# All weighted tiles of a deformable convolution summed on VectorE, partly out of PSUM, before TensorE folds them

## The reference, cut to what matters

```python
x = x + _L0_conv_ref(_gn(x), ...)   # Winograd convolution with weights of 6x6 frequencies
x = x + _L1_conv_ref(_gn(x), ...)   # offsets by a 3x3 convolution, then a deformable 3x3 convolution
x = x + _L2_conv_ref(_gn(x), ...)   # four convolutions with binary weights, activations of 8 bits
x = x + _L3_conv_ref(_gn(x), ...)   # 3x3 convolution + edge convolution, channel attention
```

```python
def qhtanh(x):
    return jnp.clip(ste_round(jnp.clip(x, -10.0, 10.0) / HT_SCALE), -127.0, 127.0) * HT_SCALE
out01 = qhtanh(out01) + qhtanh(identity0)
x_b1l0 = qhtanh(out01) + qhtanh(op1)
```

```python
diff_v = xp[:, :, :-2, :] - xp[:, :, 2:, :]
edge_out = jnp.einsum('oc,bchw->bohw', W_edge, jnp.abs(diff_v))
```

## Time and profile before

| | |
|---|---|
| device time, median of 3 runs | 4324.02 us |
| the three runs | 4323.59, 4324.02, 4336.19 us |
| span of the profiled execution (first to last instruction) | 4328.9 us |
| mean granted TensorE clock | 0.983 |
| PE busy | 4115.4 us (95%) |
| DVE busy | 3191.3 us (74%) |
| ACT busy | 1827.2 us (42%) |
| POOL busy | 3159.8 us (73%) |
| one image in the steady part, by PE's tiles | about 257 us |

### The profile page before, as it was taken

The page is one execution under the profiler, slowest core; times in us unless marked ns, Lnnn a source line. Parts: engine busy times, 40 slices in busy tenths (PEclk is TensorE's granted clock), DMA queues, the critical chain, the costliest instruction groups (busy, mean ns, idle before and its releaser), DMA issues.

```text
span 4328.9 us, 61705 instructions
## 1 busy us (share of the span) xinstructions
PE 4115.4 (95%) x21925; PEld 1924.0 (44%) x21925; DVE 3191.3 (74%) x6460; ACT 1827.2 (42%) x2008; POOL 3159.8 (73%) x3094
## 2 busy tenths in 40 slices
PE   2899999999999999999999999999999999999993
PEld 2444444444444444444444444444444444444441
DVE  4757787777877777787777877877787777877663
ACT  1344444444444434444444444444444444444431
POOL 1777777777777777777777777777777777777750
PEclk8899999999999999999999999999999999999996
DMA  4677787878878788887877878787887878878762
GB/s 111 216 234 245 238 263 220 265 227 248 256 235 263 227 250 258 245 256 229 261 233 246 270 233 261 223 251 249 245 258 232 258 234 253 260 237 258 240 194 64
DMA packets 480231, 1022.57 MB, mean 236 GB/s; under 512 B 262164, under 2 KB 298356, under 8 KB 475636
## 3 DMA queue, kind: packets, MB, share of 16 engines
q1 hardware_dynamic: 283252, 460.40, 34.7%
q10 hardware_dynamic: 98400, 356.97, 25.4%
q0 software_dynamic: 98304, 201.52, 16.5%
HBM read 862.19 MB, written 73.20 MB: 216 GB/s over the span
## 4 chain that ended last, share of the span: by engine, by line
PE 72%; DVE 13%; POOL 5%; issue 4%; DMA 3%; SPq 1%; ACTq 1%; ACT 1%; POOLq 0%; DVEq 0%
PE ps_r L1506 52%; PE ps_c L1492 5%; POOL ring L599 5%; PE ps_y L1521 4%; PE ps_a L1445 3%; DVE col_hat L1198 2%; PE ps_c L1535 2%; PE ps_a L1492 2%; DMA taps_c<-plane_act 1%; PE ps_y L1542 1%; DVE ps_w L1219 1%; DVE ring L1225 1%; PE ps_a L1483 1%; DVE ring L1221 1%; ACTq L793 1%
## 5 line engine op out<-in xcount | busy, mean ns | idle before, releaser
L599 POOL DMA_INDIRECT ring<-patch_table,idx_part x3072 | 3151.6, 1026 | 1031.6 <-issue 1019.6
L1506 PE MATMUL ps_r<-select,image 128*128 128x512 f32 x6912 | 3160.9, 602 | 21.1 <-DVE col_hat L1198 15.3
L1506 PEld LDWEIGHTS ps_r<-select,image 128*128 128x128 f32 x6912 | 1253.6, 190 | 1424.3 <-issue 1368.9
L1198 DVE TENSOR_TENSOR col_hat<-ps_r,col_hat 128x512 f32<-128x512 f32 x1152 | 790.6, 686 | 919.1 <-PE ps_r L1506 917.8
L649 ACT ACTIVATE select<-row_in,minus_row 128x1536 f32<-128x1536 f32 x384 | 604.8, 1575 | 1042.7 <-PE ps_r L1506 556.9
L651 ACT ACTIVATE select<-select,one_col 128x1536 f32<-128x1536 f32 x384 | 605.3, 1576 | 12.5
L668 ACT COPY samples<-ps_c 128x512 f32<-128x512 f32 x256 | 148.9, 582 | 655.8 <-PE ps_c L1535 655.8
L1219 DVE TENSOR_TENSOR ps_w<-ring,ps_w 128x384 f32<-128x384 f32 x512 | 284.8, 556 | 19.8 <-DMA ring<-patch_table,idx_part 15.2
L1225 DVE TENSOR_TENSOR ring<-ring,ps_w 128x384 f32<-128x384 f32 x512 | 280.3, 547 | 4.4
L1221 DVE TENSOR_TENSOR ring<-ring,ps_w 128x384 f32<-128x384 f32 x512 | 280.2, 547 | 0.0
L1521 PEld LDWEIGHTS ps_y<-col_hat,w_dense 128*32 128x32 f32 x6144 | 143.5, 109 | 297.5 <-issue 245.9
(11 more groups left out here) (233 smaller groups left out, 2588.9 us busy)
## 6 DMA issues: line engine op xcount, KB each, us to landing
col_hat<-coord_table SPq DMA_DIRECT2D x384, 768.0 KB
row_in<-coord_table ACTq DMA_DIRECT2D x384, 768.0 KB
ring<-patch_table,idx_part POOLq DMA_INDIRECT x3072
taps_c<-plane_act SPq DMA_DIRECT2D x135, 268.1 KB
coord_table<-wino ACTq DMA_DIRECT2D x64, 216.0 KB
taps_c<-xn_c ACTq DMA_DIRECT2D x96, 130.0 KB
taps_c<-xn_c SPq DMA_DIRECT2D x96, 130.0 KB
plane_act<-act_c SPq DMA_DIRECT2D x180, 65.0 KB
```

The lines of the kernel that those rows point to most:

```text
L599: nc.gpsimd.indirect_dma_start(out=ring[j][:, h % 2, k, :], out_offset=None, in_=table, in_offset=bass.IndirectOffsetOnAxis(ap=idx_part[:, ...
L1198: v.tensor_tensor(hat_t, ps_r[:, (s + t) % 2], hat_t, ALU.mult).then_inc(tile_weighed, 1)
L1506: ins = mm(ps_r[:, (s + t) % 2], image[:, m, t], select[s % 2][:, m], start=(m == 0), stop=(m == PAIRS - 1))
```

## The change

Three things are edited. All 24 slots now sum their tiles, and the sum has another form: the first tile of a slot is weighed from PSUM into SBUF as before; the second and third are multiplied in place in PSUM, and DVE then adds the PSUM tile to the sum in SBUF. `tile_weighed`, for which PE waits before it reuses the buffer and before it folds, is now raised by that addition. PE folds one tile in every slot. Second, `affine` leaves the results of convolutions 1, 2 and 3 in `ps_c`, and DVE rounds them there in two halves of 512 elements (`rounded_plus_psum`) in place of one instruction over 1024 in SBUF; three new counts (`read1` to `read3`) release the PSUM bank to PE. Third, the absolute value of the edge part goes from DVE at (21,2) to ACT, under `c_late` in slot 21, and PE waits for ACT there.

```diff
-SUMMED = (4, 5, 6, 7, 8, 11, 14, 19, 20, 21, 22, 23)
+SUMMED = range(SLOTS)
...
-LAST_READ = {8: "downb", 11: "conv1b", 14: "conv2b", 17: "conv3b", 23: "excite"}
+LAST_READ = {8: "downb", 23: "excite"}
+LAST_ROUNDED = {11: "read1", 14: "read2", 17: "read3"}
...
-                    nc.scalar.activation(t_c[:, h * HALF:(h + 1) * HALF] if i < 4 else t_d[:, h * HALF:(h + 1) * HALF],
+                    half = slice(h * HALF, (h + 1) * HALF)
+                    nc.scalar.activation({0: t_c[:, half], 4: t_d[:, half]}.get(i, ps_c[:, h]),
...
             def c_late(n, s):
+                if s == 21:
+                    act.wait_ge(c_dve.sem, c_dve.at(n, "edges"))
+                    nc.scalar.activation(t_d, t_d, ACT.Abs).then_inc(c_act.sem, 1)
...
-                hat_t = col_hat[s % 3][:, t]
-                v.tensor_tensor(hat_t, ps_r[:, (s + t) % 2], hat_t, ALU.mult).then_inc(tile_weighed, 1)
-
-            def sum_tiles(n, s, t):
-
-                hats = col_hat[s % 3]
-                dve.wait_ge(tile_weighed, (n * SLOTS + s) * WT + t + 1)
-                if t == 1:
-                    tiles_added[0] = chain.add(v.tensor_tensor(hats[:, 0], hats[:, 0], hats[:, 1], ALU.add))
+                hat_t, rows_t = col_hat[s % 3][:, t], ps_r[:, (s + t) % 2]
+                if t > 0 and s in SUMMED:
+                    chain.step(v.tensor_tensor(rows_t, rows_t, hat_t, ALU.mult))
+                    total = col_hat[s % 3][:, 0]
+                    dve.wait_ge(tile_weighed, tile)
+                    ins = v.tensor_tensor(total, total, rows_t, ALU.add)
                 else:
-                    chain.upto(tiles_added[0])
-                    v.tensor_tensor(hats[:, 0], hats[:, 0], hats[:, 2], ALU.add).then_inc(tiles_summed, 1)
+                    ins = v.tensor_tensor(hat_t, rows_t, hat_t, ALU.mult)
+                ins.then_inc(tile_weighed, 1)
...
+            def rounded_plus_psum(dst, rest):
+
+                for h in range(2):
+                    chain.add(v.tensor_scalar(ps_c[:, h], ps_c[:, h], M, M + 127.0, ALU.add, ALU.min))
+                chain.join()
+                for h in range(2):
+                    half = slice(h * HALF, (h + 1) * HALF)
+                    ins = stt(dst[:, half], ps_c[:, h], M - 127.0, rest[:, half], ALU.max, ALU.subtract)
+                    if h == 0:
+                        chain.add(ins)
+                return ins
...
-                    rounded_plus(tc_, tc_, dn)
+                    rounded_plus_psum(tc_, dn).then_inc(c_dve.sem, 1)
...
-                if at == (21, 2):
-                    chain.join()
-                    stt(td_, td_, -1.0, td_, ALU.mult, ALU.max).then_inc(c_dve.sem, 1)
...
-                    if s in SUMMED:
-                        pe.wait_ge(tiles_summed, n * len(SUMMED) + SUMMED.index(s) + 1)
-                    else:
-                        pe.wait_ge(tile_weighed, (n * SLOTS + s) * WT + t + 1)
+                    pe.wait_ge(tile_weighed, (n * SLOTS + s) * WT + (WT if s in SUMMED else t + 1))
...
-                    pe.wait_ge(c_dve.sem, c_dve.at(n, "edges"))
+                    pe.wait_ge(c_act.sem, c_act.at(n, "edges"))
```

21 lines of the change are left out of this document (11 added, 10 removed).

## The result

| | median us | range, runs | ratio to before, 95% |
|---|---|---|---|
| before | 4328.15 | 4323.59 to 4336.19, 4 | |
| changed | 4452.94 | 4449.16 to 4455.13, 4 | 1.0286 [1.0272, 1.0301] |

What follows compares the result with a forecast made beforehand. PE was taken as the bound on average, DVE in slots 8 to 10. Stretches +6.1 and edge +2.0 gave 8.1 us an image over 15 images, together +119 us: 4443 us, 8 in 10 within 4335 to 4495.

Steps and rivals of the forecast that it cites:

- The bound of each stretch: PE bounds on average, DVE in slots 8 to 10, where three sums and a rounding add 2.8 us an image.
- Slots 0 to 4: Eight added sums, 5.8 us, partly absorbed by DVE's idle and a cushion: PE 2.0 us later an image (1.5 to 4.3).
- Slots 12 to 14: Added sums and a rounding make PE wait; less two folds saved, +1.3 us an image (0.5 to 2).
- Slots 15 to 18: Early additions absorbed; delays only before PE's two averages: +0.9 us an image (0 to 1.5).
- Slots 11 and 19: The two shortened folds left over count as PE's gain: -0.9 us an image.
- The edge: Slot 21: PE waits for ACT's absolute value behind four DMA issues, +2.0 us an image (0 to 3.2).
- The sum: 8.1 us for each of 15 images, image 0 -4, the last image's end +2: together +119 us.
- (a): Rival: DVE keeps up, PE's shorter work counts, POOL's gathers get faster: -3.2 us an image, 4272 us; chance 0.11.
- (b): Rival: POOL's unchanged pace hides PE's changes within 2 us an image: 4310 to 4330 us; chance 0.09 together with (d).
- (d): Rival: only slots 8 to 10 and the edge count, other cushions hold: about 4325 us; chance 0.09 together with (b).
- (c): Rival: PE and DVE wait by turns, no idle is used: the upper sum, 4516 us; chance 0.10.
- The signs named: Right: PE busy -80 us, L1206 waits 100, DVE +280, L1290 0.69, POOL's ring full; wrong: L787 over before PE's slot 21 convolution.

Runs made afterwards that it cites:

- e3_sums: Kernel before with all 24 slots summed in the old form (sum in SBUF), nothing else changed: 4403.2 us against 4324.8, ratio 1.0183.
- e2_round: Kernel before with only the three roundings read from PSUM: 4336.4 us against 4324.8, ratio 1.0028.
- e12_swap_8: Kernel before with the new form of the sums, slots 3, 13 and 16 also summed, slot 8 no longer: 4297.3 us against 4328.4, ratio 0.9927.
- e11_no_round: Changed kernel with its roundings back in SBUF as before, sums and edge part kept: 4401.3 us, ratio to the kernel before 1.0166.
- e1_edge: Kernel before with only the edge part's absolute value moved to ACT in slot 21: 4353.9 us against 4324.8, ratio 1.0064.
- e5_no_edge: Changed kernel with the absolute value back on DVE at (21,2): 4449.0 us, ratio to the kernel before 1.0269.
- e7_fold_one: Kernel before, PE folding only the first tile in the 12 unsummed slots, their other tiles left out of the result: 4299.5 us, ratio 0.9925.

## Why the prediction was right, point by point

**The bound of each stretch.** Right. PE and DVE take turns, and what DVE gets more in slots 8 to 10 counts whole: +2.78 us for a forecast of 2.8, with PE's waits of 0.91, 1.90, 0.42 and 1.79 in it. e3_sums (+2.20 in this stretch, three sums being 2.16) and e2_round (+0.66, the rounding being 0.65) split it as the sum did. In reverse e12_swap_8 took 1.45 us off by two sums less. The price of a sum, 0.72 us, rests on the start of the product that the sum waits for. The earlier trace rows don't show it; it lies 0.72 us ahead of their L1205, at 2223.78:

```profile
2223.06 0.69 DVE L1198 TENSOR_TENSOR col_hat<-ps_r,col_hat 128x512 f32<-128x512 f32 x1
```

**Slots 0 to 4.** Right in size, +1.95 for 2.0. Of the range of 1.5 to 4.3 the lower part held: the idle between additions could be used. e3_sums shows that the sums alone do it.

**Slots 12 to 14.** +1.45 for 1.3. PE waits 1.17, 0.42 and 0.18 us there, for 1.1, 0.6 and 0.4 forecast. (The idle of DVE that the prediction reads as 1.9 us in the whole stretch is 14.79 - 12.79 = 2.0, and the row covers slots 12 and 13.) e11_no_round takes 0.67 of it back, one rounding.

**Slots 15 to 18.** Wrong: +2.54 for 0.9, above its upper end of 1.5. The step that failed is the sentence "the early additions are absorbed". In front of the transposes of slot 16 PE had a cushion of 0.66 us, and 2.1 us of additions in slot 15 stood ahead of the copies that they need: slot 16 is 1.29 us longer at full clock. Another 0.57 is the clock, a third of the images at 1.70. The second half of the term, slots 17 and 18, was about right: +0.69 for 0.9.

**Slots 11 and 19.** Forecast -0.9. The folds gave 0.44 (11.46 to 11.02) and 0.31, as told. But half of the images lose 1.70 us of clock in slot 11, which eats them: -0.05. The clock is a term that the prediction doesn't have at all: it counted PE's waits as if they cost their own length only.

**The edge.** Wrong here: +2.0 forecast, nothing measured. Alone it cost +1.38 us in slot 21 and 29 us in all (e1_edge), so the mechanism was there; the term's lower bound, that ACT's queue should come earlier by 2 us, is what happened. The prediction took the length of four DMA issues, 7.09 us, from one image of the kernel before and carried it over as if it belonged to the instructions; in the changed kernel the mean is 5.3 us. Why they became shorter isn't shown; it goes with the gathers' pauses, as said at e5_no_edge.

**The sum.** 8.1 us an image forecast, 8.5 measured; 119 us forecast on the span and 121.3 measured (4450.2 less 4328.9). Only 14 images carry the term, and not 15: the last image's tiles take 1.3 us less than before, image 0's 2.1 less (-4 forecast), and what follows the last tile takes 2.8 more (+2 forecast). The agreement is better than the reasoning, and in part luck: +1.1 in front of the transposes and +1.4 of clock were missed, and the edge's -2.1 makes up for them. Taken alone, the three parts cost 78, 12 and 29 us, in sum 119; but in the changed kernel the roundings count 52 and the edge next to nothing.

**The rivals.** (a), that DVE keeps up, is refuted by PE's waits in slots 0 to 4 (0.47 to 0.79 us in front of three folds and an average) and 8 to 10. Its second condition, faster gathers, came true all the same: the mean gather fell from 1026 to 998 ns. (b), POOL as the pace, doesn't hold in the changed kernel but does in e7_fold_one, once PE has 5.2 us less. (d), that the other cushions hold, fails: slots 0 to 4, 12 to 14 and 15 to 18 all grew. (c), the coupling without any use of idle, reached its end only in slots 15 to 18, and there by another cause.

**The signs named.** One sign of being wrong came true, for the edge part: L787 was over (2483.14) before PE had done its convolution of slot 21 (2483.89), and PE's wait there is 3.7 us in all and not 2 us an image. DVE's busy time +266 for 280, L1290 693 ns, 77 us of PE's waits for L1206: as told or nearly. PE's busy time fell by 36 us and not by 80: the folds gave 85 (L1527 has 163.5 us; L1521 had 248.4), but the tiles' rows (L1506, L1515) take 32 us more. Of these 22 lie in the twelve slots at the lower clock, whose 18 products take 12.6 to 12.7 us for 10.8; the rest are rows that the profile shows longer where PE waits in between (two sixes of 2.84 us for a twelve of 5.42). POOL's new waits are there, but mostly for the table (168.4 us in 14 waits), not for a full ring. That sign was wrong in its reason: a full ring (waits for L1234) accounts for 12.2 us, and the table that POOL gathers from is written once an image, so a slower image holds POOL there.

## What to carry to other kernels

Price an added instruction by the stretch it stands in: find for each wait of the other engine the cushion ahead of it, and go through all of them, small transposes too. Where PE is made to wait, look at its granted clock behind the wait before the wait is taken for the whole price. Work that is moved between two engines which take turns is to be placed slot by slot: sums in all slots cost this kernel 1.8%, and in the slots in which DVE had room they are part of a version that is 0.7% faster; parts measured alone don't add, since each uses slack that the others need.
